# A two-layer graph network on one core: the last layer's rows in four blocks of 512 columns, with squares about a first-half mean and one root

## The reference, cut to what matters

```
h = x @ W                                    # 256 x 1024
al, ar = h @ a_l, h @ a_r
e = exp(-leaky_relu(al[src] + ar[dst], 0.1))
rowsum = segment_sum(e, src)
h_prime = segment_sum(e[:, None] * h[dst], src) / (rowsum[:, None] + 1e-5)
y = x + elu(h_prime)
out = (y - mean(y)) / sqrt(var(y) + 1e-5)    # per row of 1024
```

## Time and profile before

| | us |
|---|---|
| median of 3 runs (lowest, highest) | 337.24 (336.33, 338.43) |
| the profiled execution's own time | 337.25 |
| its span, first to last instruction | 335.3 |
| mean granted TensorE clock | 0.985 |
| busy in the span: PE, DVE, ACT, POOL | 316.2, 280.9, 188.2, 125.3 |
| the rest of the time after PE's last product (ended about 325.2) | 10.1 |

### The profile page before, as it was taken

How to read it: one execution, slowest core, us unless ns; L and a number is a source line. 1 busy time by engine, 2 the same in 40 slices (tenths; PEclk the granted TensorE clock), 3 DMA queues, 4 the chain that set the end, 5 groups by cost and what they waited for, 6 DMA issues and landing times.

```text
span 335.3 us, 4498 instructions
## 1 busy us (share of the span) xinstructions
PE 316.2 (94%) x1438; PEld 243.4 (73%) x1438; DVE 280.9 (84%) x415; ACT 188.2 (56%) x286; POOL 125.3 (37%) x127
## 2 busy tenths in 40 slices
PE   8999999999999999889899999999999999999970
PEld 8778877776664678658788878888787686788730
DVE  0998999998969989979899899889888977883644
ACT  3764594323016336777786687656248676841355
POOL 4200032058000492727998799794000300005000
PEclk9999999999999999979999999999999999999996
DMA  6999599969998999311713332004697997000003
GB/s 219 401 406 411 201 334 368 355 244 203 278 360 297 379 419 410 158 63 22 167 64 65 64 127 97 31 26 102 195 368 230 344 394 283 3 1 0 2 1 125
DMA packets 19351, 68.86 MB, mean 205 GB/s; under 512 B 2413, under 2 KB 2413, under 8 KB 19329
## 3 DMA queue, kind: packets, MB, share of 16 engines
q1 hardware_dynamic: 13536, 50.07, 39.8%
q0 software_dynamic: 3232, 12.41, 13.7%
q10 hardware_dynamic: 2560, 6.10, 5.4%
HBM read 63.31 MB, written 5.26 MB: 205 GB/s over the span
## 4 chain that ended last, share of the span: by engine, by line
PE 48%; DVE 37%; DMA 5%; ACT 5%; issue 4%; POOL 0%; DVEq 0%; POOLq 0%; ACTq 0%
DVE ps L1179 10%; PE ps L1550 9%; PE ps L1673 7%; PE ps L1382 7%; PE ps L1431 6%; DVE W_lo L912 6%; PE ps L1602 6%; DMA W_raw<-in_L_gnn_W_oo_dram 5%; PE ps L1610 2%; DVE tile_val L931 2%; PE ps L1705 2%; PE ps L1637 2%; PE ps L1559 2%; DVE B_tab L1110 2%; PE ps L1415 1%
## 5 line engine op out<-in xcount | busy, mean ns | idle before, releaser
L581 ACT CAST W_hi<-W_raw 128x1024 fp32r<-128x1024 f32 x62 | 63.0, 1047 | 48.4 <-DMA W_raw<-in_L_gnn_W_ho_dram 25.1
L1179 DVE SCALAR_TENSOR_TENSOR ps<-ps,wa_bc 128x1024 f32<-128x1024 f32 x58 | 69.2, 1252 | 5.7 <-PE ps L1550 5.7
L912 DVE TENSOR_TENSOR W_lo<-W_raw,W_hi 128x1024 fp32r<-128x1024 f32 x54 | 66.0, 1255 | 6.4 <-ACT W_hi L581 4.0
L1382 PE MATMUL ps<-W_hi,xT_hi 128*128 128x512 f32 x112 | 45.8, 409 | 0.8 <-DVE W_lo L912 0.8
L1550 PE MATMUL ps<-A_tab,oh 128*128 x116 | 42.5, 448 | 3.0 <-DVE ps L1179 3.0
L1382 PE MATMUL ps<-W_lo,xT_hi 128*128 128x512 f32 x112 | 43.7, 390 | 0.0
L1550 PE MATMUL ps<-B_tab,oh 128*128 x116 | 37.4, 404 | 1.7 <-DVEq L905 1.7
L1382 PE MATMUL ps<-W_hi,xT_lo 128*128 128x512 f32 x112 | 34.6, 390 | 0.0
L487 POOL TENSOR_SCALAR sc<-sc 128x256 f32<-128x256 f32 x29 | 28.4, 978 | 2.6
L1431 PE MATMUL ps<-W_raw,hh_x 128*128 128x512 f32 x64 | 28.2, 594 | 0.0
L1550 PEld LDWEIGHTS ps<-B_tab,oh 128*128 128x128 f32 x116 | 22.2, 192 | 7.0 <-issue 2.2
(11 more groups left out here) (333 smaller groups left out, 643.2 us busy)
## 6 DMA issues: line engine op xcount, KB each, us to landing
W_raw<-in_L_gnn_W_ho_dram SPq DMA_DIRECT2D x8, 1024.0 KB, 7.8
W_raw<-in_L_gnn_W_hh_dram SPq DMA_DIRECT2D x8, 1024.0 KB, 8.9
W_raw<-in_L_gnn_W_hn_dram SPq DMA_DIRECT2D x8, 1024.0 KB, 5.6
W_raw<-in_L_gnn_W_on_dram SPq DMA_DIRECT2D x8, 1024.0 KB, 6.8
W_raw<-in_L_gnn_W_oo_dram SPq DMA_DIRECT2D x7, 1024.0 KB, 12.2
W_raw<-in_L_gnn_W_dram SPq DMA_DIRECT2D x4, 1024.0 KB, 7.1
table_scratch<-tabs ACTq DMA_DIRECT2D x2, 1024.0 KB, 6.7
key_rows<-key_rows_scratch POOLq DMA_DIRECT2D x1, 1792.0 KB, 13.1
```

Source lines behind the costliest of these rows:

```text
L581: sa.copy(halves(n)[0], W_raw[:, n // 2 % NS, n % 2, :]).then_inc(hi_made, 1)
L912: v.tensor_tensor(lo, W_raw[:, n // 2 % NS, n % 2, :], hi.bitcast(F32), ALU.subtract).then_inc(lo_made, 1)
L1179: v.scalar_tensor_tensor(acc, acc, 0.0, wa_bc[:], ALU.max, ALU.mult, accum_out=keys[:, t, 2:3]).then_inc(reduced, 1)
L1382: ins = mm(acc[:, m * D + f:m * D + f + 512], x_part(n - first, m), W[:, f:f + 512], start=(n == first and x_part is hi and W is W1), stop ...
```

## The change

PE's products stay as they are, but the two pieces of row block 0 have a stage each, so that there are four, `hp0` to `hp3`. ACT takes exp and relu of each piece apart, and between them the squares of row block 0 in two pieces, as soon as DVE has them; their scratch output goes to x_nat. Those of row block 1 follow the load of the root's table. DVE works in four pieces; after the first of each row block it makes `less_first`, the negative mean of 512 numbers. The means, the drift between the two means and the variance are computed for both row blocks in operations of two columns, and one root serves both. `out0` now comes after `scale3`.

```diff
-                     "x1T0a", "x1T0b", "x1T1", "h_0", "h_1", "albc", "sums", "hp0", "hp1", "hp2"]
+                     "x1T0a", "x1T0b", "x1T1", "h_0", "h_1", "albc", "sums", "hp0", "hp1", "hp2", "hp3"]
...
-            act.wait_ge(pe_step, pe_at("hp0"))
-            act.wait_ge(dve_step, dve_at("row_sums"))
-            exponential(0, 0, D)
-            positive(0, 0, D)
-            for part, (a, b) in ((1, (0, 512)), (2, (512, D))):
-                act.wait_ge(pe_step, pe_at(f"hp{part}"))
-                exponential(1, a, b)
-                positive(1, a, b)
+            def block_squares(h, k, ready):
+
+                act.wait_ge(dve_step, dve_at(ready))
+                own = slice(k * 512, (k + 1) * 512)
+                sa.activation(x_nat[:, h, own], y1[:, h, own], ACT.Square,
+                              bias=less_first[:, h:h + 1], accum_out=squares[:, 2 * h + k:2 * h + k + 1]).then_inc(squared, 1)
+
+            for i in range(4):
+                act.wait_ge(pe_step, pe_at(f"hp{i}"))
+                if i == 0:
+                    act.wait_ge(dve_step, dve_at("row_sums"))
+                exponential(i // 2, i % 2 * 512, (i % 2 + 1) * 512)
+                positive(i // 2, i % 2 * 512, (i % 2 + 1) * 512)
+                if i == 1:
+                    block_squares(0, 0, "y0a")
+                if i == 2:
+                    block_squares(0, 1, "y0b")
             warm_up(ACT.Sqrt, 0)
-            act.wait_ge(dve_step, dve_at("mean2"))
-            deviation(0, h1[:, 0, :])
-            root(0, 1, 3)
-            act.wait_ge(dve_step, dve_at("mean3"))
-            deviation(1, h1[:, 1, :])
-            root(1, 2, 4)
+            block_squares(1, 0, "y1a")
+            block_squares(1, 1, "y1b")
+            act.wait_ge(dve_step, dve_at("variance"))
+            sa.activation(deviations[:, 0:2], variances, ACT.Sqrt, bias=eps_ln[:, 0:1], scale=1.0 / D).then_inc(act_step, 1)
...
-            elu_and_add(0, 0, D, "h_exp0", "h_relu0", y_sums[:, 0:1])
-            mean(0, "mean2")
-            elu_and_add(1, 0, 512, "h_exp1", "h_relu1", y_sums[:, 2:3])
-            elu_and_add(1, 512, D, "h_exp2", "h_relu2", y_sums[:, 3:4])
-            link(v.tensor_tensor(y_sums[:, 1:2], y_sums[:, 2:3], y_sums[:, 3:4], ALU.add))
-            mean(1, "mean3")
-            inverse(0, 1, "sd2")
+            for h in range(2):
+                for k in range(2):
+                    i = 2 * h + k
+                    elu_and_add(h, k * 512, (k + 1) * 512, f"h_exp{i}", f"h_relu{i}", y_sums[:, i:i + 1])
+                    if k == 0:
+                        link(v.tensor_scalar(less_first[:, h:h + 1], y_sums[:, i:i + 1], -1.0 / 512, None, ALU.mult))
+                    stage(f"y{h}{'ab'[k]}")
+
+
+            firsts, seconds = (y_sums[:, 0:4].rearrange("p (h k) -> p h k", k=2)[:, :, k] for k in range(2))
+            link(v.tensor_tensor(less_mean[:, 2:4], firsts, seconds, ALU.add))
+            link(v.tensor_scalar(less_mean[:, 0:2], less_mean[:, 2:4], -1.0 / D, None, ALU.mult))
+            link(v.tensor_tensor(drift, less_mean[:, 0:2], less_first, ALU.subtract))
+            link(v.tensor_tensor(drift, drift, drift, ALU.mult))
+            dve.wait_ge(squared, 6)
+            firsts, seconds = (squares[:, 0:4].rearrange("p (h k) -> p h k", k=2)[:, :, k] for k in range(2))
+            link(v.tensor_tensor(variances, firsts, seconds, ALU.add))
+            link(v.scalar_tensor_tensor(variances, drift, -float(D), variances, ALU.mult, ALU.add))
+            stage("variance")
+            inverse(0, 2, "sd2")
+            link(v.tensor_scalar(small[:, 10:11], less_mean[:, 1:2], rstd[:, 1:2], None, ALU.mult))
+            stage("scale3")
             normalise(y2[:, 0, :], y1[:, 0, :], 0)
             stage("out0")
-            inverse(1, 2, "sd3")
-            link(v.tensor_scalar(small[:, 10:11], less_mean[:, 1:2], rstd[:, 1:2], None, ALU.mult))
-            stage("scale3")
             normalise(y2[:, 1, 0:512], y1[:, 1, 0:512], 1)
             stage("out1")
...
                     ins = hp(0, n, hd)
-            stage(ins, "hp0")
+                    if hd:
+                        stage(ins, f"hp{n}")
             for n in range(2):
                 for hd in range(2):
                     ins = hp(1, n, hd)
-                stage(ins, f"hp{1 + n}")
+                stage(ins, f"hp{2 + n}")
```

More of the change, by code:

```diff
@@ L126, in gnn_two_layers @@
         slopes = small[:, 14:16]
+        less_first, drift, variances = (small[:, k:k + 2] for k in (16, 18, 20))
         eps_ln = sb("eps_ln", [P, 1])
@@ L357, in gnn_two_layers @@
         PE_STAGES = ["xT0a", "xT0b", "xT1", "totals", "x_rowsT", "perm0", "perm1", "keysT", "hoB_0", "hoB_1", "PT", "zT0", "zT1", "q1", "shift0", "shift1",
-                     "x1T0a", "x1T0b", "x1T1", "h_0", "h_1", "albc", "sums", "hp0", "hp1", "hp2"]
+                     "x1T0a", "x1T0b", "x1T1", "h_0", "h_1", "albc", "sums", "hp0", "hp1", "hp2", "hp3"]
         ACT_STAGES = ["xT0a", "xT0b", "xT1", "hh_x", "ooB_out", "C_hh", "C_oo", "A_rows0", "A_rows1", "L_oo", "L_hh", "static0", "static1", "B_rows0", "B_rows1", "counts", "parts", "rescale", "soft0", "soft1", "zT0", "both0", "zT1",
                       "both1", "q0_low", "q1_low", "sd0", "x1T0a", "sd1", "x1T0b", "x1T1", "h1_0", "h1_1a",
-                      "exp0", "exp1", "h1_1", "h_exp0", "h_relu0", "h_exp1", "h_relu1", "h_exp2", "h_relu2", "sd2", "sd3", "out3"]
+                      "exp0", "exp1", "h1_1", "h_exp0", "h_relu0", "h_exp1", "h_relu1", "h_exp2", "h_relu2", "h_exp3", "h_relu3", "sd2", "out3"]
         DVE_STAGES = ["xT0a", "xT0b", "xT1", "tot", "totals", "columns", "ooA_out", "placed0", "placed1", "keys", "key_u8", "hoA_b",
@@ L364, in gnn_two_layers @@
                       "zT1", "mean0", "x1_0a", "x1T0a", "x1_0b", "mean1", "x1_1", "x1T0b", "x1T1", "dots0", "dots1a", "al", "dots1",
-                      "ET0", "ET1", "row_sums", "mean2", "mean3", "out0", "scale3", "out1"]
+                      "ET0", "ET1", "row_sums", "y0a", "y0b", "y1a", "y1b", "variance", "scale3", "out0", "out1"]
         def pe_at(s):
```

## The result

| | before | changed |
|---|---|---|
| median of the runs, us | 337.24 (9 runs, 336.33 to 338.43) | 339.08 (9 runs, 338.27 to 339.90) |
| ratio of the runs, 95% interval | | 1.0044 (1.0030 to 1.0058) |
| profiled execution, its span | 337.25, 335.3 | 338.27, 336.5 |

The change makes the kernel slower by 0.44%, 1.0 to 2.0 us by the interval, which is inside the 1% that the prediction calls no change. The medians are 1.84 us apart, the ratio says 1.5.

What follows compares the result with a forecast made beforehand. ACT, the fuller engine beside DVE, bounds the last stretch, then the stores. 0.04 won, 0.44 lost and the stores' burst make the last landing 1.90 later: 337.25 becomes 339.15, forecast 339.1, range 337.5 to 340.7.

Steps and rivals of the forecast that it cites:

- part 2: ACT until the squares are done: squares of 0.83, done at 330.60 against 330.64; gain up to here 0.04, which is none.
- rival A: Final stores: each takes what its size took, whatever runs beside it; last landing +1.24, time 338.5; chance 0.2.
- Part 1: Start of row block 0's exponentials: hp0 releases ACT at 320.92 and not 321.78, 0.86 earlier.
- Part 3: Last square to root: two small DVE operations now stand between, root at 331.08 against 330.64, +0.44.
- Part 4: Final stores: all 1.05 MB go in one burst of some 2.7 us, landing at 336.82, +1.90 against 334.92.
- B: ACT's squares: 512 columns take 1.25 like 1024, not 0.83; four cost 1.7 more, 340.8; chance 0.07.
- C: Squares at the lower bound 0.59 and stores by latency: 337.5, the time of before, not slower; chance 0.08.
- D: ACT's first square, ahead of the third exp, waits longer for y0a: about 1.1 us, 340.2; chance 0.05.

Runs made afterwards that it cites:

- before_four_pieces: Kernel before with only PE's stages, exp, relu and DVE's passes in four pieces; squares, means and roots as before; ratio to before 1.0009.
- after_squares_last: Changed kernel with both squares of row block 0 moved behind the table load; ratio to before 1.0054.
- after_first_store_early: Changed kernel, but SP's first 512 KB store takes row block 0 from before the layer norm (y1), once y1b is told; ratio to before 1.0009.
- pool_statistics: Changed kernel with squares about zero, GpSimd making mean and root bias by five small operations, own root and early store for row block 0; ratio to before 1.0009.

## Why the prediction was right

**The forecast**, 339.1 with "same", is what came: the median is 339.08. That it fits so closely is in part luck. The ratio says 1.5 us and the profile 1.4, where I had said 1.9; the difference is part 2's, below. By the time alone rival A (1.24 us, 338.5) is as near as the forecast. What decides is how the stores behaved. Two of the signs that I had named did not come either: squares of 0.8 to 0.85 and a root 0.4 later than before.

**Part 1** was right to the hundredth: the first exp 0.86 earlier.

**Part 2** had the right order of events, and its prices were too high. The first square starts at T+3.71, to the hundredth as forecast (323.49 - 319.78), after ACT had stood idle for 0.33 and not 0.19. From there on I counted 0.83 for a square with its sum, and it takes 0.70 to 0.72. The 0.21 for the read came from the one place where the next instruction waits for the read's result, the root; where none waits, the read costs 0.10. Three squares make 0.36, and an exp and relu with ready work behind them took 1.05 and not 1.19 (324.06 to 325.11), 0.14. ACT's last read ends at T+10.28, where I had T+10.82 (330.60 - 319.78): 0.5 earlier. The account of the 0.86 was right in kind: before_four_pieces shows that PE's fourth piece makes the early start worthless alone, and after_squares_last that the squares in the gaps win 0.7 of it. I had all of it eaten by the dearer squares and activations, and 0.5 was left when the last read ended.

**Part 3** was priced at 0.44; from the end of the last read to the root it is 0.55 (329.91 to 330.46) where it was 0.03 (330.61 to 330.64), so 0.52. It eats what part 2 had left: the root is where it was, and not 0.44 later.

**Part 4** was right, and is the result. The burst took 2.7 us, and my sum from the first issue on holds: 332.13 + 1.36 + 2.7 = 336.19, against 336.15. All three stores were issued 0.5 before my times, by part 2's error, and the last landing is 1.4 later than before and not 1.9. Two experiments that move only the first store account for 1.1 of it and for 1.3 of it. What remains, 0.1 to 0.3, goes with the last issue, which is 0.8 later than before (T+13.32 against T+12.54). With the first store out of the way that costs little: in after_first_store_early the last store lands at T+15.3, against T+15.1 before.

**The rivals.** A, stores by latency: fell with both store experiments. The time of a 256 KB store went from 2.0 to 3.6 us, by what was moving beside and ahead of it. The Trainium skill (DMA: Bandwidth & Descriptors, Anatomy of one DMA) gives a cost by size alone, for transfers issued by GpSimd, which these are not; by its figures 256 KB are an estimated 2.6 us and 512 KB 3.2. The runs come near it for a 256 KB store with little beside it (2.0 to 2.6), not for the 512 KB alone (2.6), and not for a 256 KB store behind others in the burst (3.2 to 3.6). B, dear squares, and C, squares at 0.59: neither; 0.71 lies between. D, the hold-up by the first square: `y0a` came when I had said, ACT waited 0.33 for it, and after_squares_last shows that moving the square away is no gain.

## What to carry to other kernels

Look at what a merged step hands to the queue behind it. One root for two blocks saved an instruction of 0.3 us and made a store of 512 KB wait 1.9 us, until it moved together with the last two. And an early start into a chain whose pieces are released at fixed times is worth what can be put into the gaps, no more.

## What was unexpected in the hardware

GpSimd's operations on one column took 0.68 to 0.81 us when they began during DVE's two-input passes of 512 columns, seven of them in two kernels, and 0.19 to 0.21 while DVE stood still. Rows of pool_statistics, the same operation for both row blocks, the first during a pass of DVE, the second after them all:

```profile
325.55 0.75 DVE L1367 SCALAR_TENSOR_TENSOR y<-y,small 128x512 f32<-128x512 f32 x1
325.66 0.73 POOL L570 TENSOR_SCALAR small<-small 128x1 f32<-128x1 f32 x1
...
329.89 0.21 POOL L570 TENSOR_SCALAR small<-small 128x1 f32<-128x1 f32 x1
```

Each of the seven ends 0.04 to 0.20 us after the DVE pass in which it began (here 326.39 against 326.30). So they look less like slow operations than like operations that waited for the pass to end, though that is not shown. One does not fit: at 323.94, with a pass that had started at 323.92, GpSimd took 0.19. That it is DVE's work which holds them is read from the times at which they fall together; no run varied it alone. The second surprise is the 0.10 us for reading a sum, when nobody waits for it.
